# One VectorE operation that takes each routed slot's result out of the bank, another buffer for slot 0's result, and two weight roundings moved within their rounds

## What is computed

```
logits = xf @ gate_w                       # 4096 rows, 8 experts
top_logits, top_idx = top_k(logits, 2)     # two experts per row
h     = gelu(einsum('nd,edh->neh', xf, w1) + b1)      # H = 256
out_e = einsum('neh,ehd->ned', h, w2) + b2
routed = einsum('ne,ned->nd', gates, out_e)
x = x + gb * (routed + shared)             # gb: one row of 512 for each sequence
```

## Time and profile before

| | us |
|---|---|
| median of 3 runs | 1965.56 (1963.47 to 1968.12) |
| the profiled execution's own time | 1966.27 |
| its span (first to last instruction) | 1964.5 |
| from the first L881 of round 1 to the end of the span | 255.85 |
| from there to the last L881 (rounds 1 to 67 begin in it) | 236.55 |
| the store of `r_t` before the first slot's result, issued | 1708.91 |

### The profile page before, as it was taken

One profiled execution on the slowest core, in us unless ns is written; L12 is line 12 of the kernel. 1 busy time (PEld: TensorE's weight loads), 2 busy tenths in 40 slices (PEclk: granted clock), 3 DMA queues, 4 the chain that ended last, 5 costly groups with the idle time before them and its releaser, 6 DMA issues.

```text
span 1964.5 us, 26328 instructions
## 1 busy us (share of the span) xinstructions
PE 1914.0 (97%) x8850; PEld 1537.8 (78%) x8850; DVE 1279.6 (65%) x2764; ACT 706.1 (36%) x1412; POOL 277.7 (14%) x251
## 2 busy tenths in 40 slices
PE   7999999999999999999999999999999999999998
PEld 4687778878888888888887787787787677688886
DVE  5689989875455545556265356366366676488887
ACT  4576776531111111123112222212223343355554
POOL 0000000000000000000000011011020220377775
PEclk9999999999999999999999999999999999999999
DMA  5313211141101210124111321311233554578886
GB/s 185 135 44 121 75 60 33 50 140 65 65 22 43 75 65 22 43 77 163 51 65 54 98 67 55 120 66 54 99 109 135 180 183 176 173 142 155 154 153 97
DMA packets 86688, 189.97 MB, mean 97 GB/s; under 512 B 9525, under 2 KB 26198, under 8 KB 81516
## 3 DMA queue, kind: packets, MB, share of 16 engines
q1 hardware_dynamic: 62988, 127.77, 19.1%
q0 software_dynamic: 23568, 60.51, 14.3%
HBM read 118.56 MB, written 72.12 MB: 97 GB/s over the span
## 4 chain that ended last, share of the span: by engine, by line
PE 87%; DVE 6%; issue 3%; POOL 2%; ACT 1%; DMA 1%; POOLq 0%; SPq 0%; DVEq 0%; ACTq 0%
PE bank L651 12%; PE bank L653 12%; PE bank L652 12%; PE bank L656 12%; PE bank L658 11%; PE bank L657 11%; PE bank L894 3%; PE bank L821 1%; POOL out L615 1%; PE bank L670 1%; PE bank L896 1%; PE bank L922 1%; PE bank L924 1%; PE bank L923 1%; PE bank L881 1%
## 5 line engine op out<-in xcount | busy, mean ns | idle before, releaser
L651 PE MATMUL bank<-x_hi,w_blk 128*128 128x512 f32 x1024 | 403.1, 394 | 3.4 <-DVE s_t L1581 3.4
L653 PE MATMUL bank<-x_hi,w_blk 128*128 128x512 f32 x1024 | 399.4, 390 | 0.0
L652 PE MATMUL bank<-x_lo,w_blk 128*128 128x512 f32 x1024 | 398.9, 390 | 0.0
L1581 DVE TENSOR_TENSOR s_t<-act_t,bank 128x512 f32<-128x512 f32 x128 | 87.8, 686 | 302.6 <-PE bank L653 298.4
L1182 ACT ACTIVATE s_hi<-s_t 128x512 fp32r<-128x512 f32 x128 | 80.9, 632 | 441.1 <-DVE s_t L1581 411.8
L651 PEld LDWEIGHTS bank<-x_hi,w_blk 128*128 128x128 f32 x1024 | 192.7, 188 | 42.8 <-DVE w_blk L1376 3.0
L653 PEld LDWEIGHTS bank<-x_hi,w_blk 128*128 128x128 f32 x1024 | 192.4, 188 | 40.7
L652 PEld LDWEIGHTS bank<-x_lo,w_blk 128*128 128x128 f32 x1024 | 192.8, 188 | 38.9
L656 PE MATMUL bank<-w_blk,s_hi 128*128 128x512 f32 x512 | 200.6, 392 | 0.0
L1180 ACT ACTIVATE act_t<-bank 128x512 f32<-128x512 f32 x128 | 76.3, 596 | 343.3 <-PE bank L653 343.3
L658 PE MATMUL bank<-w_blk,s_lo 128*128 128x512 f32 x512 | 199.4, 389 | 0.0
(11 more groups left out here) (264 smaller groups left out, 3500.9 us busy)
## 6 DMA issues: line engine op xcount, KB each, us to landing
x_t<-y_scratch SPq DMA_DIRECT2D x24, 1024.0 KB, 4.9
residual<-r_t SPq DMA_DIRECT2D x16, 1024.0 KB, 4.3
r_t<-residual SPq DMA_DIRECT2D x16, 1024.0 KB
raw<-w_swi POOLq DMA_DIRECT2D x16, 768.0 KB, 4.5
y_scratch<-y_t SPq DMA_DIRECT2D x32, 256.0 KB, 2.7
r_t<-x_tok SPq DMA_DIRECT2D x8, 1024.0 KB
h_rows<-hrow SPq DMA_DIRECT2D x32, 256.0 KB
y_scratch<-hT SPq DMA_DIRECT2D x8, 1024.0 KB, 4.0
```

Source lines behind the costliest of these rows:

```text
L651: nc.tensor.matmul(dst, w[:, 0, col:col + P], rhs_hi, start=start, stop=False)
L652: nc.tensor.matmul(dst, w[:, 0, col:col + P], rhs_lo, start=False, stop=False)
L653: return nc.tensor.matmul(dst, w[:, 1, col:col + P], rhs_hi, start=False, stop=stop)
L1581: nc.vector.tensor_tensor(s_t[:, s % 2, :], act_t[:, s % 2, :], bank[4 + (2 * s + 1) % 3][:, :], ALU.mult).then_inc(f.s_ok, 1)
```

## The change

ScalarE's `slot_o` is removed, with its 71 operations L1311 and the semaphore `rt.og_ok`. VectorE's L1955 becomes one operation that reads the bank itself, multiplies with the gate of each row, and with `gb_row`; it waits for `rt.dn`. `slot_down(j)` now waits for `rt.o_ok`, VectorE's report on slot j-2. The list of `o_t` is reordered: slot 0 (and 10, 20, ...) uses 180 KB, slot 1 uses 164 KB, so that the wait for `out_st` moves from slot 0 to slot 1. `late_rows` names the same four places as before. On ScalarE `piece_hi` of rounds 1 and 3 goes from the end of the round to its begin. VectorE's `piece_lo` stays at the round's end.

```diff
-        o_t = [at(f"o_t{i}", k, [P, D]) for i, k in enumerate((164, 166, 168, 170, 180, 182, 128, 130, 132, 134))]
+        o_t = [at(f"o_t{i}", k, [P, D]) for i, k in enumerate((180, 164, 166, 168, 170, 182, 128, 130, 132, 134))]
-        late_rows = [o_t[4], o_t[5], p_t[0], p_t[1]]
+        late_rows = [o_t[0], o_t[5], p_t[0], p_t[1]]
...
@@ slot_down, PE
-                    pe.wait_ge(rt.og_ok, j - 1)
+                    pe.wait_ge(rt.o_ok, j - 1)
...
@@ ScalarE
-            def slot_o(j):
-
-                act.wait_ge(rt.dn, j + 1)
-                if j >= 2:
-                    act.wait_ge(rt.o_ok, j - 1)
-                nc.scalar.activation(p_t[j % 2][:, :], bank_o[j % 2][:, :], ACT.Copy,
-                                     scale=gate_t[:, j:j + 1]).then_inc(rt.og_ok, 1)
...
             for j in range(NSLOT):
+                if j in R_TURNS:
+                    piece_hi(R0 + 14 + R_TURNS.index(j))
                 if j + 3 < NSLOT:
                     slot_x(j + 3)
...
-                slot_o(j)
-                if j in R_TURNS:
-                    piece_hi(R0 + 14 + R_TURNS.index(j))
...
@@ slot_o, VectorE
-                dve.wait_ge(rt.og_ok, j + 1)
-                if j == 0:
+                dve.wait_ge(rt.dn, j + 1)
+                if j == 1:
 
                     dve.wait_ge(out_st, 16 * NT)
...
-                nc.vector.tensor_tensor(o_t[j % NO][:, :], p_t[j % 2][:, :], gb_row[:, :],
-                                        ALU.mult).then_inc(rt.o_ok, 1)
+                nc.vector.scalar_tensor_tensor(out=o_t[j % NO][:, :], in0=bank_o[j % 2][:, :], scalar=gate_t[:, j:j + 1],
+                                               in1=gb_row[:, :], op0=ALU.mult, op1=ALU.mult).then_inc(rt.o_ok, 1)
```

More of the change, by code:

```diff
@@ L278, in build @@
         settled, sc_go = sem("settled"), sem("sc_go")
-        rt = sems("routed", "tr_ok xh_ok xl_ok up u1_ok u_ok gl_ok gt_ok gh_ok gl_lo dn og_ok gr_ok o_ok")
+        rt = sems("routed", "tr_ok xh_ok xl_ok up u1_ok u_ok gl_ok gt_ok gh_ok gl_lo dn gr_ok o_ok")
         PASS = {"b": 0, "c": 1, "s": 2}
@@ L1304, in slot_g @@
                 nc.scalar.activation(gT_hi[:, j % 2, :], bank_g[j % 2][:, 0:H], ACT.Copy).then_inc(rt.gh_ok, 1)
-            def slot_o(j):
-                act.wait_ge(rt.dn, j + 1)
-                if j >= 2:
-                    act.wait_ge(rt.o_ok, j - 1)
-                nc.scalar.activation(p_t[j % 2][:, :], bank_o[j % 2][:, :], ACT.Copy,
-                                     scale=gate_t[:, j:j + 1]).then_inc(rt.og_ok, 1)
-            bank_o = bank[2:4]
             slot_x(0)
```

## The result

The changed kernel takes 1957.63 us (median of 8 runs, 1955.21 to 1960.44), the kernel before 1965.61 us in the runs beside it (8 runs, 1963.47 to 1968.38): a ratio of 0.9961 with a 95% interval of 0.9951 to 0.9970. That is 8.0 us faster; 6.0 us and 1959.6 us were forecast. A later comparison gave 1957.43 us (7 runs) against 1963.39 (28 runs), ratio 0.9973 (0.9962 to 0.9984), which is 6.0 us.

A forecast was written before the change was run, and what follows sets the result against it. TensorE, busy 97% of the span, was taken as the bound, with time to gain only where it stands still. Start 5.7 us plus end 0.3 us gave 6.0 us, so 1965.56 - 6.0 = 1959.6 us, range 1956.6 to 1963.2.

The forecast's parts named there:

- (a): VectorE at the start: slot 0's result no longer waits for the store, gain 2.91 us; slot 1's cover is 1.5 us.
- (b): VectorE in rounds 1 and 3: `piece_hi` at the round's begin removes waits before L1376, gain 1.75 + 1.76 = 3.51 us.
- (c): ScalarE's `xT_hi` behind the moved rounding delays VectorE's `xT_lo`: cost 0.2 us in round 1, 0.3 us in round 3.
- (d): New VectorE operation takes 749 ns, 0.06 us more each, 0.2 us over slots 0 to 3; upper bound 1.22 us.
- rival D: VectorE becomes the bound if the new operation exceeds 0.93 us; at 1.22 us the time is 1978 us; chance 0.04.
- The sum of the start: Rounds 1 to 5: 2.91 + 3.51 - 0.2 - 0.3 - 0.2 = 5.7 us gained.
- The end: Last rounds: slot 68's result need not wait for `p_t`, so POOL's last scatters come 0.3 us earlier.
- The clock: TensorE's half-clock stretch in 1716 to 1719 lies in VectorE's shadow, its going adds nothing; full clock expected after.
- A: Whole kernel, as computed: gain 5 to 7 us, 1958.6 to 1960.6 us; chance 0.68.
- E: More than computed: pieces cost nothing and TensorE regains other waits, gain 7 to 9 us; chance 0.03.
- B: Start partly given back to another wait (ScalarE's `slot_x`, late store, gathered rows): gain 3.7 us, 1961.8 us; chance 0.20.
- C: Start gains nothing, TensorE waits for something unchanged and VectorE only for it: 0 to 1 us, 1965 us; chance 0.05.

The follow-up runs named there:

- experiment 9: Changed kernel with a second VectorE operation like the one forming `gb_row` in every slot, written to an unread buffer; 1987.07 us against 1963.99, ratio 1.0114.
- experiment 2: Kernel before with only the two `piece_hi` roundings moved to the round's begin on ScalarE; 1960.71 us against 1963.39, ratio 0.9989.
- experiment 3: Kernel before with slot 0's other buffer and the pieces first, ScalarE's copy kept; 1957.83 us against 1963.39, ratio 0.9977.
- Experiment 7: Changed kernel with both roundings in round 0, ahead of slot 2's gelu on ScalarE; 1957.42 us, ratio 0.9972.
- experiment 1: Kernel before with slot 0's result in the other buffer alone, store wait at slot 1; 1961.13 us against 1963.39, ratio 0.9989.
- experiment 4: Kernel before with the new VectorE operation alone, buffers and places of the pieces as before; 1962.09 us against 1963.39, ratio 0.9992.
- experiment 6: Changed kernel with the two roundings put back to the round's end on ScalarE; 1959.64 us against 1963.39, ratio 0.9981.
- experiment 8: Changed kernel with both roundings in round 0 and the two `piece_lo` remainders on GpSimd; 1959.49 us against 1963.39, ratio 0.9983.
- experiment 11: Kernel before with slot 0's other buffer alone, run once more; 1960.25 us in one run.

## Why the prediction was right, point by point

- **The bound.** TensorE sets the middle, and only its standing still at the start is to be had. The middle took 210.63 us against 210.65, and experiment 9 shows the margin that makes it so.
- **(a) Slot 0's wait.** Gain forecast 2.91 us, measured 3.69 - 0.79 = 2.90 us on VectorE. Such a close hit holds for this pair of profiles: in the second profile of the kernel before `gb_row` came later after the L881 and the pair was 3.02 us apart, which makes the gain 2.23 us. The store ends the wait at its own time, so what stands before it is hidden in the kernel before and not in the changed one. The wait is hidden at slot 1, with 1.15 us to spare instead of the 1.5 forecast.
- **(b) The pieces.** Forecast 3.51 us, measured 1.75 + 1.77 = 3.52 us.
- **(c) What stands behind them on ScalarE.** Forecast 0.5 us of cost, measured none in the changed kernel: `xT_hi` was always there in time. In round 3 it was ready at 1714.85 + 0.58 = 1715.43, and VectorE, without its own wait of 0.38 us (next point), would have been there at 1715.34, so about 0.1 us was hidden. With ScalarE's copy kept the wait is there, 0.67 and 0.24 us in experiments 2 and 3. Experiment 7 agrees: freeing ScalarE of both roundings gives nothing measurable.
- **Not forecast:** VectorE waited 0.95 instead of 0.44 us before slot 0's `gb_row` and 0.38 us before slot 2's, 0.9 us together, without a releaser in the profile. Step (a) had said that nothing in the change moves the first L1943; against the L881 of round 1 it came 0.45 us later (2.84 us instead of 2.39). The first is not the change's doing: it was 0.96 us, and the distance 2.85 us, in the second profile of the kernel before, and over the profiles of all kernels it varied from 0.20 to 0.96 us. The second does go with the change: it is 0.38 and 0.39 us in both profiles of the changed kernel and 0.45 us in experiment 3, and it is in no profile of the kernel before, nor of experiments 1, 2, 4 and 6. What either wait is stays open.
- **(d) The new operation.** Forecast 749 ns, measured 751, as long as L1933 with the same form from SBUF. The prediction says that the trace has no operation that reads a bank, a scalar by partition and a tensor. That is wrong: the first block of the kernel before has one 32 times, before the stretch from which the earlier trace rows were taken.

```profile
L1471 DVE SCALAR_TENSOR_TENSOR kv_t<-bank,r_pair,w_t 128x512 f32<-128x512 f32 x32 | 23.8, 743 | 0.0
```

So the price could be read beforehand, and the upper bound of 1.22 us with the worst case of rival D was not needed. The 65 ns more (an estimate from 62 cycles) that the Trainium skill ("VectorE: DVE Perf Modes", section on the TRN2 errata) gives an operation reading PSUM do not show: 751 against 751 ns. What the new operation gains by itself is not shown either: 0.7 us alone (experiment 4) and 0.4 us on top of the other two edits (experiment 3) are within the spread.
- **The sum of the start.** Forecast 5.7 us, measured 5.40. In VectorE's terms 2.90 + 3.52 + 0.09 (`p_t` at slot 2) - 0.24 (four operations) - 0.89 = 5.38 us. Term (c) was too dear by 0.5, and 0.9 us of unexplained waits were not counted. That the sum missed by only 0.3 us is therefore in part luck: two errors of opposite sign stand in it.
- **The end.** Forecast 0.3 us; the last scatter came 0.27 us nearer to the last L881. It landed later, with 7.08 us from its start to the end of the span instead of 6.92, so 0.11 us reached the end. Over more profiles it is nearer to the forecast: from the last L881 to the end of the span it is 18.70 to 19.49 us (mean 19.01) in six profiles with the new operation (both of the changed kernel, experiments 4, 6, 7 and 8), and 19.20 to 19.49 us (mean 19.33) in six without it. The two groups overlap.
- **The clock.** That the slow stretch lay in VectorE's shadow is right for the kernel before, and so it carried no term. But the reason is narrower than it was put: in experiments 1 and 11 the same half clock falls in round 5, out of the shadow, and takes 1.6 of 2.4 us back. The changed kernel has no gap of over 0.61 us and keeps its clock; with the pieces last again (experiment 6) it has gaps of 1.79 and 1.64 us and keeps it too.
- **8.0 or 6.0 us.** The slots give 5.4 to 6.3 us by two profiles on each side. The clock of the first 200 us differs from run to run and shifts the slots by up to 5 us. The changed kernel's 8 times in the first comparison show it: four are 1955.2 to 1955.8 us with a mean granted clock of 0.994 or 0.995, four 1959.5 to 1960.4 us with 0.991 or 0.992, and the median of 1957.63 lies in the empty space between. So a median of 8 runs can easily be off by 2 us. That the surplus of the first comparison is this alone is likely, but not shown.
- **Rivals.** By the stretch and by the later comparison A came. The first comparison's 8.0 us by itself lies in E's band (7 to 9 us, chance 0.03), but the reason given there does not hold: the start gained 5.4 us and not more than computed. B's wait on ScalarE or for gathered rows does not appear in the changed kernel; on ScalarE it does in experiments 2 and 3. C falls with experiments 2 and 3, and with TensorE following VectorE by 2.4 us in experiment 1. D falls with 751 ns; experiment 9 shows what it would have been.

## What to carry to other kernels

When an engine ahead of the bound is late for a few rounds, add up its own waits on the path from the last point that doesn't move to the operation that lets the bound go; removed together they counted nearly in full here (5.4 of 6.4 us), and one alone was largely paid back by a slower clock. Put a wait for a transfer on the first item whose turn comes after its landing, not on the first item. And before crediting a change with a gain, cut the span where the changed code begins: here half of the difference between the first two profiles lay ahead of it. Before setting a bound on an operation whose form seems new, look for that form in the whole trace and not only in the stretch that changes.

## What the runs showed of the hardware

- A VectorE operation beside two tensor operations of GpSimd on 128x1024 elements took 4.19 instead of 0.75 us and ended 0.56 us after the second of them (experiment 8). Both of its tensor inputs were in SBUF.
- The granted clock fell to half right behind one gap of TensorE of 2.35 and 2.62 us (both profiles of the kernel before), 2.40 (experiment 2), 2.89 (experiment 4) and 3.88 us (experiment 8). It did not fall behind 2.32 and 2.28 us (experiments 1 and 11), but there it fell behind the next gap, of 2.09 and 2.07 us, 9 us later. A gap of 2.08 us that came 15 us after the first, in both profiles of the kernel before, left it at full, and so did gaps of 1.79 and 1.64 us, 9 us apart (experiment 6). What decides between these is not shown.
- GpSimd's gather issue took 1.26 us in most of the changed kernel's middle rounds instead of 1.11 (medians 1258 and 1109 ns), with the same transfers. With 1.58 us for the scatter and twice 0.30 us its round is 3.44 us, right below TensorE's 3.453. It cost nothing here, and was not looked into.
